# Early-fusion block on one core: full-height table products, high halves read in place, and reordered queues

## The chip, the cores and the metric

One core of one Trainium2 chip. The metric is the device time of one execution in microseconds (us). Several executions are timed and the median is given; one more execution is recorded by the profiler.

## What is computed

The block has three stages. With `x` of 8 x 3 x 512 x 192 and `txt` of 8 x 128 x 192:

```python
h = tokenizer(x)                      # sines and cosines of 6 bands, times W: 8 x 512 x 192
h = concat([h, txt], axis=1)          # 8 x 640 x 192: 40 tiles of 128 tokens
h = h + attention(layernorm(h))
h = h + soft_experts(layernorm(h))

def attention(x):                     # 12 heads of 64, 4 query groups
    k, v = x @ Wk, x @ Wv
    q = ln(gelu((x @ Wq) @ Wt + bt)) * gt + betat       # per group and head, over 64
    qf, kf = phi(q) / sqrt(128), phi(k)                 # phi(u) = [relu(u), relu(-u)]
    kv, ksum = sum_n kf v, sum_n kf                     # one table per batch and head
    out = (qf @ kv) / (qf . ksum + 1e-6)
    return gelu(ln(out @ Wf + bf)) @ Wo + bo
```

Matrix products of float32 are made from bf16 halves: a x b is taken as a_hi b_hi + a_hi b_lo + a_lo b_hi, summed in PSUM.

## The kernel before

`early_fusion_kernel` calls the tokenizer, `attention_weights` (folds Wt into Wq), `keys_and_values`, `attend` and `soft_experts` one after the other. Each writes the instruction streams of the five engines by hand, with semaphores between them; an engine runs its own stream strictly in the order written. The change touches `keys_and_values` and `attend`.

**keys_and_values** goes over 8 batches x 5 tiles x 2 halves of six heads. For each half TensorE projects keys and values into a bank pair of `ps_p` (two sets, one for each half), ScalarE writes `kf` = relu(+k), relu(-k) and `v_hi`, VectorE and GpSimd make `kf_hi`, `kf_lo`, `v_lo`. One half tile later `accumulate` (L521 to L534) sums the tables: for each pair of heads, each sign and each of the three half products, two matmuls, one per head (`side`), with 64 columns of weights each. They write the lower or upper 64 partitions of `ps_kv`, so the table of a head lies on 64 partitions, two signs apart in the free dimension. A 65th column of ones in `v` gives `ksum`. That makes 36 matmuls for each of the 80 half tiles. `store_kv` splits the finished sums into `kvs` (high and low bf16).

**attend** works through 40 tiles x 6 octets (8 heads of the 48 query heads, as 4 pairs) in slots. `slot(tile, j)` exists for each engine, and names in which order that engine touches the neighbouring octets:

- TensorE (from L969): queries of octet j+3 (5 matmuls of 512 columns), at j = 2 `turn_x`, then `turn_octet(j)` (4 f32 transposes of the normalised queries into `ps_t`), at j = 4 `turn_y` of the previous tile (6 transposes), `attend_octet(j-1)`, `fuse(j-2)` (24 matmuls of 384 columns with Wf), `turn_outputs(j-1)` (4 transposes into `ps_u`), at j = 5 `project_out`(18 matmuls).
- ScalarE: `high_outputs(j-2)` (`o_hi`), `gelu(j+3)`, `features(j)` (L1006: `phi` = relu(+-q gt +- betat); one instruction for each sign and query group, so two, or four in octets 1 and 4 in which two groups meet), `square(j+2)`, at j = 4 both parts of `fused_gelu`.
- VectorE: `center(j+2)` (L1090), `low_outputs(j-2)` (`o_lo`, L1134), `sum_q(j+3)`, `divide(j-1)`, `scale_q(j+1)`, `high_phi(j)` (L1112, cast of `phi` to `phi_hi`), `sum_squares(j+2)`; in single slots the layernorms of `x` and `y`, and at j = 5 `high_ys` (L1163).
- GpSimd: `rstd_q(j+1)` (L1221, L1224), `low_phi(j)` (L1231), in single slots `rstd_y` and `low_ys`.

Features of sign +1 and -1 lie apart in the free dimension, and the two heads of a pair on 64 partitions each. So a table product contracts over 64 rows. The two heads go to the two halves of the array's rows and to two banks:

```python
for n, (feature, table) in enumerate(((phi_hi, 0), (phi_hi, 1), (phi_lo, 0))):
    for a in range(2):
        rows = slice(a * DH, (a + 1) * DH)
        last = nc.tensor.matmul(
            ps_o[:, a, i * KVW:(i + 1) * KVW],
            feature[rows, j % 2, sign, i * P:(i + 1) * P], kv_now[rows, table, pair, sign, :],
```

That is 4 pairs x 2 signs x 3 x 2 = 48 matmuls an octet, 65 columns each. `kv_now` holds the tables of the tile's batch: SyncE copies 390 KB in all 40 times from `kvs` by DMA (L854), so that TensorE's operands have fixed addresses. `phi`, `phi_hi` and `phi_lo` have two buffers (j % 2); `ps_t`, `ps_o`, `ps_u` one each. `fuse(j-2)` waits for `o_hi` and `o_lo` of its octet (L935).

The tokenizer, which the change leaves alone, reads high halves in place: `high(r)` (L72) is the float32 tile `feat` seen as bf16, every second element, and goes to L154 as weights; the low halves `f_low` are packed bf16 and go to L163.

## Time and profile before

| | |
|---|---|
| median of 3 runs | 2654.25 us (2653.22 to 2655.28) |
| profiled execution | 2652.76 us |
| its span, first to last instruction | 2651.0 us |
| TensorE busy / VectorE / ScalarE / GpSimd | 94% / 91% / 52% / 51% of the span |
| mean granted TensorE clock | 0.965 of full speed |
| keys_and_values | about 510 to 760 us |
| attend | about 760 to 2530 us |

Engines in the rows below: PE is TensorE's matmuls, PEld its weight loads, DVE VectorE, ACT ScalarE, POOL GpSimd. A matmul's recorded time is a latency and overlaps the next one's, so for TensorE the start times tell the pace. "<-issue" marks idle time in which the engine waited for nothing that the profile shows.

### The profile page before, as it was taken

The page shows a single profiled execution, that of the slowest core. Times are in us where ns is not written, and L with a number is a line of the kernel's source. Part 1 is how long each engine was busy: PE and PEld are TensorE (multiplying, and loading weights), DVE is VectorE, ACT ScalarE, POOL GpSimd, SP SyncE. Part 2 cuts the span into 40 slices and gives each one's busy share as a digit, 9 for nine tenths or more (in the row PEclk, how much of TensorE's full clock was granted, in tenths as well). Part 3 has the DMA queues.
Part 4 walks back from the last instruction along what each step waited for, and adds up shares of the span by engine and source line. Part 5 has one row for each costly group of instructions (what it writes and reads, how often), then busy time and mean ns, then how long its engine had stood idle before and what let it go on. Part 6 is the DMA issues. An engine that isn't in the chain of part 4 may idle for free. (4 is left out here: it accounts for less than half of the span.)

```text
span 2651.0 us, 74429 instructions
## 1 busy us (share of the span) xinstructions
PE 2481.3 (94%) x29338; PEld 1697.5 (64%) x29338; DVE 2419.1 (91%) x3549; ACT 1385.3 (52%) x2270; POOL 1351.4 (51%) x1019
## 2 busy tenths in 40 slices
PE   4999999788879999999999999999999999999946
PEld 2777777555546666666666666666666666666634
DVE  6999999788879999999999999999999999999852
ACT  5677767455554454555545454545454545454441
POOL 0000000455556666666666666666666666666630
PEclk8999999799989999999999999999999999999965
DMA  7421210111100000000000000000000000000001
GB/s 149 105 54 36 53 36 18 51 39 45 36 14 14 7 12 6 12 6 12 6 12 6 12 6 12 6 12 6 12 6 12 6 12 6 12 6 12 8 7 60
DMA packets 45459, 62.41 MB, mean 24 GB/s; under 512 B 4736, under 2 KB 36480, under 8 KB 45080
## 3 DMA queue, kind: packets, MB, share of 16 engines
q1 hardware_dynamic: 44248, 61.09, 8.7%
q8 instruction: 41, 0.67, 0.1%
q10 hardware_dynamic: 1152, 0.51, 0.1%
q14 instruction: 18, 0.15, 0.0%
HBM read 41.67 MB, written 3.93 MB: 17 GB/s over the span
## 5 line engine op out<-in xcount | busy, mean ns | idle before, releaser
L1231 POOL TENSOR_TENSOR phi_lo<-phi,phi_hi 128x1024 bf16<-128x1024 f32 x240 | 511.4, 2131 | 459.8 <-DVE phi_hi L1112 459.8
L1022 ACT ACTIVATE o_hi<-ps_u 128x512 bf16<-128x512 f32 x240 | 143.3, 597 | 706.1 <-PE ps_u L927 706.1
L941 PE MATMUL ps_y<-staging,o_hi 128*128 128x384 bf16 x1920 | 470.7, 327 | 9.8 <-DVE o_lo L1134 1.9
L941 PE MATMUL ps_y<-staging,o_lo 128*128 128x384 bf16 x1920 | 469.3, 326 | 0.0
L941 PE MATMUL ps_y<-wf_lo,o_hi 128*128 128x384 bf16 x1920 | 469.2, 326 | 0.0
L1224 POOL TENSOR_TENSOR q_ssq<-q_ssq,half 128x8 f32<-128x8 f32 x240 | 405.9, 1691 | 18.8
L1013 ACT ACTIVATE phi<-ps_t,betat,gt 128x512 f32<-128x512 f32 (+1 forms) x640 | 384.5, 672 | 0.9 <-PE ps_t L896 0.8
L1090 DVE SCALAR_TENSOR_TENSOR shared<-q_sum,shared 128x512 f32<-128x512 f32 x240 | 374.5, 1560 | 1.4
L154 PE MATMUL acc<-w_b,feat 128*128 128x384 bf16 x1728 | 295.6, 331 | 42.7 <-DVE w_b L266 39.3
L154 PEld LDWEIGHTS acc<-w_b,feat 128*128 128x128 bf16 x1728 | 168.4, 99 | 158.3 <-DVE w_b L266 39.9
L941 PEld LDWEIGHTS ps_y<-staging,o_lo 128*128 128x128 bf16 x1920 | 187.8, 98 | 124.3
L941 PEld LDWEIGHTS ps_y<-wf_lo,o_hi 128*128 128x128 bf16 x1920 | 187.4, 98 | 124.5
L941 PEld LDWEIGHTS ps_y<-staging,o_hi 128*128 128x128 bf16 x1920 | 169.3, 98 | 118.9 <-issue 15.6
L369 POOL MEMSET half<- 128x40 f32 x1 | 0.1, 131 | 476.6 <-POOLq L101 476.6
L252 DVE TENSOR_TENSOR f_low<-feat 128x4608 bf16<-128x4608 f32 x48 | 237.7, 4952 | 1.4 <-ACT feat L196 1.4
L997 ACT ACTIVATE shared<-ps_a 128x512 f32<-128x512 f32 x240 | 143.3, 597 | 179.2 <-PE ps_a L880 176.2
L1112 DVE CAST phi_hi<-phi 128x1024 bf16<-128x1024 f32 x240 | 219.9, 916 | 0.0
L914 PE MATMUL ps_o<-kv_now,phi_hi 64*128 64x65 bf16 x7680 | 212.9, 191 | 1.7 <-issue 1.7
L914 PEld LDWEIGHTS ps_o<-kv_now,phi_hi 64*128 64x128 bf16 x7680 | 183.9, 95 | 42.1 <-issue 42.1
L914 PE MATMUL ps_o<-kv_now,phi_lo 64*128 64x65 bf16 x3840 | 202.8, 190 | 0.0
L1085 DVE TENSOR_REDUCE q_sum<-shared 128x8 f32<-128x512 f32 x240 | 162.5, 677 | 20.8 <-ACT shared L997 19.6
L914 PEld LDWEIGHTS ps_o<-kv_now,phi_lo 64*128 64x128 bf16 x3840 | 180.7, 94 | 0.0
(214 smaller groups left out, 5474.2 us busy)
## 6 DMA issues: line engine op xcount, KB each, us to landing
kv_now<-kvs SPq DMA_DIRECT2D x40, 390.0 KB, 2.6
xt<-in_x_dram SPq DMA_DIRECT2D x32, 320.0 KB, 5.6
wf_f<-in_wf_dram SPq DMA_DIRECT2D x24, 384.0 KB, 3.1
xt<-in_x_dram SPq DMA_DIRECT2D x32, 256.0 KB, 6.0
out_dram<-h SPq DMA_DIRECT2D x8, 480.0 KB, 4.6
staging<-in_wq_t_dram SPq DMA_DIRECT2D x1, 3072.0 KB, 10.5
staging<-in_tok_w_dram SPq DMA_DIRECT2D x12, 192.0 KB, 8.8
staging<-in_kv_w_dram SPq DMA_DIRECT2D x1, 1536.0 KB, 14.9
```

The costliest lines, as they stand in the source:

```text
L154: last = nc.tensor.matmul(acc[:, u, t, 0:2 * DIM], high(ring(u, i))[:, k, t * P:(t + 1) * P], w_b[:, i, k, :], start=i == 0 and k == 0, st ...
L252: nc.vector.tensor_tensor(low[:, r], feat[:, r], high(r), ALU.subtract).then_inc(low_ready, 1)
L914: last = nc.tensor.matmul(ps_o[:, a, i * KVW:(i + 1) * KVW], feature[rows, j % 2, sign, i * P:(i + 1) * P], kv_now[rows, table, pair, sign ...
L941: last = nc.tensor.matmul(ps_y[:, n, 0:HC], lhs, w[part][:, c, n * HC:(n + 1) * HC], start=c == 0 and lhs is oh and part == 'wf_hi', stop= ...
L997: nc.scalar.activation(q[:, j % RING].rearrange("p h d -> p (h d)"), ps_a[:, bank[f"oct{j}"], 0:OC], ACT.Gelu).then_inc(s["gelu_done"], 1)
L1013: last = nc.scalar.activation(phi[:, j % 2, sign, a * P:b * P], ps_t[:, a * P:b * P], ACT.Relu, bias=w['betat'][:, sign, g:g + 1], scale=w ...
L1022: nc.scalar.activation(o_hi[:, j % 2], ps_u[:, 0:OC], ACT.Copy).then_inc(s["o_hi_done"], 1)
L1085: nc.vector.tensor_reduce(total[:, j % 2], q[:, j % RING], AX_X, ALU.add).then_inc(s["q_sum"], 1)
L1090: nc.vector.scalar_tensor_tensor(out=q[:, j % RING], in0=total[:, j % 2].unsqueeze(2).broadcast_to([P, OCT, DH]), scalar=1.0 / DH, in1=q[: ...
L1112: nc.vector.tensor_copy(phi_hi[:, j % 2], phi[:, j % 2]).then_inc(s["phi_hi_done"], 1)
L1224: nc.gpsimd.tensor_tensor(ssq[:, j % 2], ssq[:, j % 2], w['half'][:, 0:OCT], ALU.pow).then_inc(s["q_rstd"], 1)
L1231: nc.gpsimd.tensor_tensor(phi_lo[:, j % 2], phi[:, j % 2], phi_hi[:, j % 2], ALU.subtract).then_inc(s["phi_lo_done"], 1)
```

## The change

- `accumulate` and `attend_octet` use full-height operands: the two signs of one head together make 128 rows. 18 instead of 36 matmuls for each half tile, 24 instead of 48 for each octet, all with 128 x 128 weights and 65 columns. The tables are stored as `kv_hi`, `kv_lo` of [128, batch, head, 65].
- `attend_octet` reads `kv_hi[:, b, hd, :]` and `kv_lo` directly, with the batch `b` computed from the loop's tile; `kv_now`, its DMA and SyncE's stream in `attend` are gone.
- `features` writes one head's plus and minus features on 64 partitions each, which takes an instruction for each head, sign and group: four or eight an octet. `phi_done` rises once for each head.
- `phi_hi` and `ys_hi` become views (upper 16 bits of the float32 elements). `high_phi` and `high_ys` are gone. `low_phi` is two instructions, one for each head of the pairs (128x512 each).
- Orders: ScalarE's `square` goes ahead of `gelu` and `features`, and `fused_gelu(0)` ahead of `features`; VectorE's `sum_squares` goes up behind `low_outputs`, `y_aggregate` up, `normalize_x` from j = 1 to j = 0; TensorE turns the first half of y ahead of `turn_octet` and the second behind `attend_octet`.

```diff
@@ accumulate
-                    for j in range(HH // 2):
-                        for sign in range(2):
-                            for n, (k, v) in enumerate(((kf_hi, v_hi), (kf_hi, v_lo), (kf_lo, v_hi))):
-                                for side in range(2):
-                                    c = 2 * j + sign
-                                    last = nc.tensor.matmul(
-                                        ps_kv[side * DH:(side + 1) * DH, hf, c * KVW:(c + 1) * KVW],
-                                        k[:, m, 2 * j + side, sign, :], v[:, m, 2 * j + side, :],
...
+                    for j in range(HH):
+                        for n, (k, v) in enumerate(((kf_hi, v_hi), (kf_hi, v_lo), (kf_lo, v_hi))):
+                            last = nc.tensor.matmul(ps_kv[:, hf, j * KVW:(j + 1) * KVW],
+                                                    k[:, m, j].rearrange("p s d -> p (s d)"), v[:, m, j, :],
...
@@ attend
+        ys_hi = y.bitcast(BF16)[:, 1::2]
-        kv_now = sb("kv_now", [P, 2, HP, 2, KVW], BF16)
-        phi = sb("phi", [P, 2, 2, PAIRS * P], F32)
-        phi_hi = sb("phi_hi", [P, 2, 2, PAIRS * P], BF16)
-        phi_lo = sb("phi_lo", [P, 2, 2, PAIRS * P], BF16)
+        phi = sb("phi", [P, 2, PAIRS, 2, P], F32)
+        phi_hi = phi[:, :, :, :, :].bitcast(BF16)[:, :, :, :, 1::2]
+        phi_lo = sb("phi_lo", [P, 2, PAIRS, 2, P], BF16)
-        ys_hi = sb("ys_hi", [P, INNER], BF16)
...
-            @block.sync
-                def tables(tile):
-                    if (n := earlier(tile, NO - 1, NO, NO)) is not None:
-                        sp.wait_ge(s["attended"], n)
-                    sp.dma_start(kv_now[:, :, :, :, :], kvs[:, batch_of(tile.t)]).then_inc(s["kv_in"], 16)
...
                 def attend_octet(tile, j):
-                    pe.wait_ge(s["phi_hi_done"], count(tile, j, NO))
-                    pe.wait_ge(s["phi_lo_done"], count(tile, j, NO))
                     if (n := earlier(tile, j, NO, 1)) is not None:
                         pe.wait_ge(s["o_done"], n)
-                    if j == 0:
-                        pe.wait_ge(s["kv_in"], 16 * count(tile, 0, 1))
...
+                    b = batch_of(tile.t)
+                    for n in range(OCT):
+                        if n % PAIRS == 0:
+                            pe.wait_ge(s["phi_lo_done"], count(tile, 2 * j + n // PAIRS, 2 * NO))
+                        i = 2 * (n % PAIRS) + n // PAIRS
+                        hd = (OCT * j + i) % HEADS
+                        c = i % PAIRS
+                        out = ps_o[:, i // PAIRS, c * KVW:(c + 1) * KVW]
+                        ph, pl = (v[:, j % 2, i // 2, i % 2, :] for v in (phi_hi, phi_lo))
+                        nc.tensor.matmul(out, ph, kv_hi[:, b, hd, :], start=c == 0, stop=False, skip_group_check=True)
+                        nc.tensor.matmul(out, ph, kv_lo[:, b, hd, :], start=False, stop=False, skip_group_check=True)
+                        last = nc.tensor.matmul(out, pl, kv_hi[:, b, hd, :], start=False, stop=c == PAIRS - 1,
+                                                skip_group_check=True)
...
@@ TensorE slot
+                    if j == 4 and tile.prev().real:
+                        turn_y(tile.prev(), 0, tile)
                     if tile.real:
                         turn_octet(tile, j)
-                    if j == 4 and tile.prev().real:
-                        turn_y(tile.prev(), tile)
                     of, k = octet(tile, j - 1)
                     if of.real:
                         attend_octet(of, k)
+                    if j == 4 and tile.prev().real:
+                        turn_y(tile.prev(), 1, tile)
@@ ScalarE
-                        act.wait_ge(s["phi_hi_done"], n)
-                        act.wait_ge(s["phi_lo_done"], n)
-                    for sign in range(2):
+                        act.wait_ge(s["attended"], n)
+                    for head in range(2):
+                        rows = slice(head * DH, (head + 1) * DH)
                         for g, a, b in groups(j):
-                            last = nc.scalar.activation(
-                                phi[:, j % 2, sign, a * P:b * P], ps_t[:, a * P:b * P], ACT.Relu,
-                                bias=w['betat'][:, sign, g:g + 1], scale=w['gt'][:, sign, g:g + 1])
-                    last.then_inc(s["phi_done"], 1)
+                            for sign in range(2):
+                                last = nc.scalar.activation(
+                                    phi[sign * DH:(sign + 1) * DH, j % 2, a:b, head, :],
+                                    ps_t[rows, a * P:b * P].rearrange("p (i n) -> p i n", n=P), ACT.Relu,
+                                    bias=w['betat'][rows, sign, g:g + 1], scale=w['gt'][rows, sign, g:g + 1])
+                        last.then_inc(s["phi_done"], 1)
...
@@ GpSimd
-                    nc.gpsimd.tensor_tensor(phi_lo[:, j % 2], phi[:, j % 2], phi_hi[:, j % 2],
-                                            ALU.subtract).then_inc(s["phi_lo_done"], 1)
+                    for head in range(2):
+                        pool.wait_ge(s["phi_done"], count(tile, 2 * j + head, 2 * NO))
+                        nc.gpsimd.tensor_tensor(phi_lo[:, j % 2, :, head], phi[:, j % 2, :, head], phi_hi[:, j % 2, :, head],
+                                                ALU.subtract).then_inc(s["phi_lo_done"], 1)
```

## Rows read from the trace of the kernel before

**Rows 1.** Busy us by stage (PE, PEld, DVE, ACT, POOL, clock, DMA): two windows.

```profile
510.00:777.00 267.00, 224.07 (x3795) 143.50 (x3795) 216.71 (x434) 144.26 (x335) 143.08 (x136) 0.93 0.12 38
1200.00:2400.00 1200.00, 1194.42 (x14688) 808.61 (x14687) 1166.19 (x1809) 595.35 (x1149) 805.05 (x576) 1.00 0.02 9
```

**Rows 2.** Who waited for whom, 1200 to 2400 us (total us, times, longest).

```profile
POOL phi_lo L1231 <- DVE phi_hi L1112: 315.3, 138, 4.2
PEld ps_o L914 <- issue: 27.3, 164, 0.2
PEld ps_a L952 <- ACT shared L997: 6.1, 27, 0.2
```

**Rows 3.** Timeline of TensorE through one octet (start us, us, engine, line, ...).

```profile
1300.49 0.60 PE L896 MATMUL ps_t<-ident,z 128*128 128x128 f32 x4
1301.02 0.24 PE L914 MATMUL ps_o<-kv_now,phi_hi 64*128 64x65 bf16 x4
...
1301.75 0.19 PE L914 MATMUL ps_o<-kv_now,phi_lo 64*128 64x65 bf16 x2
1301.87 0.50 PE L941 MATMUL ps_y<-staging,o_hi 128*128 128x384 bf16 x2
...
1305.78 0.60 PE L927 MATMUL ps_u<-ident,o 128*128 128x128 f32 x4
1306.22 0.38 PE L876 MATMUL ps_a<-q_hi,xh 128*128 128x512 bf16 x1
```

**Rows 4.** Timeline of TensorE: once a tile, and two tiles 43.73 us apart.

```profile
1307.30 0.38 PE L887 MATMUL ps_a<-ident,xn 128*128 128x128 f32 x2
...
1308.77 0.19 PE L914 MATMUL ps_o<-kv_now,phi_lo 64*128 64x65 bf16 x2
1309.04 0.49 PE L941 MATMUL ps_y<-staging,o_hi 128*128 128x384 bf16 x2
...
1334.86 0.25 PE L962 MATMUL ps_a<-wo_hi,ys_hi 128*128 128x192 bf16 x1
...
1336.34 0.38 PE L876 MATMUL ps_a<-q_hi,xh 128*128 128x512 bf16 x1
...
1351.03 0.38 PE L887 MATMUL ps_a<-ident,xn 128*128 128x128 f32 x2
```

**Rows 5.** Timeline of VectorE: the low half that `fuse` at 1309.04 us reads.

```profile
1308.26 0.68 DVE L1134 TENSOR_TENSOR o_lo<-ps_u,o_hi 128x512 bf16<-128x512 f32 x1
```

**Rows 6.** Weight loads of the whole run by line and shape.

```profile
L914 PEld LDWEIGHTS ps_o<-kv_now,phi_lo 64*128 64x128 bf16 x3840 | 180.7, 94 | 0.0
L154 PEld LDWEIGHTS acc<-w_b,feat 128*128 128x128 bf16 x1728 | 168.4, 99 | 158.3 <-DVE w_b L266 39.9 <-ACT feat L195 7.4 <-issue 7.0
L163 PEld LDWEIGHTS acc<-w_b,f_low 128*128 128x128 bf16 x1728 | 144.0, 98 | 6.1
L927 PEld LDWEIGHTS ps_u<-ident,o 128*128 128x128 f32 x960 | 120.4, 142 | 21.9 <-DVE o L1126 1.4
```

**Rows 7.** Timeline of TensorE through one half tile of keys and values.

```profile
603.75 0.22 PE L529 MATMUL ps_kv<-v_hi,kf_hi 128*64 128x65 bf16 x2
...
604.31 0.20 PE L529 MATMUL ps_kv<-v_hi,kf_lo 128*64 128x65 bf16 x2
604.44 0.34 PE L510 MATMUL ps_p<-shared,xh 128*128 128x384 bf16 x1
```

**Rows 8.** Groups of VectorE and GpSimd, 1200 to 2400 us.

```profile
L1112 DVE CAST phi_hi<-phi 128x1024 bf16<-128x1024 f32 x165 | 153.9, 933 | 0.0
L1231 POOL TENSOR_TENSOR phi_lo<-phi,phi_hi 128x1024 bf16<-128x1024 f32 x165 | 351.6, 2131 | 315.3 <-DVE phi_hi L1112 315.3
```

**Rows 9.** Timeline of ScalarE: features in two and in four instructions, gelu of y.

```profile
1301.18 1.93 ACT L1013 ACTIVATE phi<-ps_t,betat,gt 128x256 f32<-128x256 f32 x4
...
1308.41 1.44 ACT L1013 ACTIVATE phi<-ps_t,betat,gt 128x512 f32<-128x512 f32 x2
...
1324.53 2.22 ACT L1037 ACTIVATE shared<-ps_a,betaf,gf 128x128 f32<-128x128 f32 x6
```

More of the change, by code:

```diff
@@ L439, in keys_and_values @@
     HH = HEADS // 2
-    PH = HH // 2
     HC = HH * DH
@@ L705, in _, with attend @@
                     batch(b, False)
-def attend(nc, w, shared, kvs, stats, h, ident):
+def attend(nc, w, shared, kv_hi, kv_lo, stats, h, ident):
     OCT = 8
@@ L892, in turn_octet @@
                     pe.wait_ge(s["q_scaled"], count(tile, j, NO))
-                    if (n := earlier(tile, j, NO, 1)) is not None:
+                    if (n := earlier(tile, 2 * j, 2 * NO, 1)) is not None:
                         pe.wait_ge(s["phi_done"], n)
@@ L901, in attend_octet @@
                 def attend_octet(tile, j):
-                    pe.wait_ge(s["phi_hi_done"], count(tile, j, NO))
-                    pe.wait_ge(s["phi_lo_done"], count(tile, j, NO))
                     if (n := earlier(tile, j, NO, 1)) is not None:
                         pe.wait_ge(s["o_done"], n)
-                    if j == 0:
-                        pe.wait_ge(s["kv_in"], 16 * count(tile, 0, 1))
-                    for i in range(PAIRS):
-                        pair = (PAIRS * j + i) % HP
-                        for sign in range(2):
-                            for n, (feature, table) in enumerate(((phi_hi, 0), (phi_hi, 1), (phi_lo, 0))):
-                                for a in range(2):
-                                    rows = slice(a * DH, (a + 1) * DH)
-                                    last = nc.tensor.matmul(
-                                        ps_o[:, a, i * KVW:(i + 1) * KVW],
-                                        feature[rows, j % 2, sign, i * P:(i + 1) * P], kv_now[rows, table, pair, sign, :],
-                                        start=i == 0 and sign == 0 and n == 0,
-                                        stop=i == PAIRS - 1 and sign == 1 and n == 2, skip_group_check=True)
+                    b = batch_of(tile.t)
[11 more added lines that the diff above has]
+                                                skip_group_check=True)
                     last.then_inc(s["attended"], 1)
@@ L1044, in slot @@
                         high_outputs(of, k)
+                    of, k = octet(tile, j + 2)
+                    if of.real:
+                        square(of, k)
                     of, k = octet(tile, j + 3)
@@ L1049, in slot @@
                         move_x(tile.next())
+                    if j == 4 and tile.prev().real:
+                        fused_gelu(tile.prev(), 0)
                     if tile.real:
                         features(tile, j)
-                    of, k = octet(tile, j + 2)
-                    if of.real:
-                        square(of, k)
                     if j == 4 and tile.prev().real:
-                        fused_gelu(tile.prev(), 0)
                         fused_gelu(tile.prev(), 1)
@@ L1106, in scale_q @@
                                             ALU.mult).then_inc(s["q_scaled"], 1)
-                def high_phi(tile, j):
-                    dve.wait_ge(s["phi_done"], count(tile, j, NO))
-                    if (n := earlier(tile, j, NO, 2)) is not None:
-                        dve.wait_ge(s["attended"], n)
-                    nc.vector.tensor_copy(phi_hi[:, j % 2], phi[:, j % 2]).then_inc(s["phi_hi_done"], 1)
                 def divide(tile, j):
@@ L1157, in normalize_y @@
                     nc.vector.tensor_scalar(y, y, yst[:, 0:1], yst[:, 1:2], ALU.subtract, ALU.mult).then_inc(s["y_norm"], 1)
-                def high_ys(tile):
-                    dve.wait_ge(s["ys_done"], count(tile, 1, 2))
-                    if (n := earlier(tile, 0, 1, 1)) is not None:
-                        dve.wait_ge(s["out_proj"], n)
-                    nc.vector.tensor_copy(ys_hi[:, :], ys).then_inc(s["ys_hi_done"], 1)
                 def add_to_h(tile):
@@ L1183, in slot @@
                         low_outputs(of, k)
+                    if j == 3 and prev.real:
+                        y_aggregate(prev)
                     if j == 0 and prev.prev().real:
                         add_to_h(prev.prev())
+                    of, k = octet(tile, j + 2)
+                    if of.real:
+                        sum_squares(of, k)
                     if j == 2 and nxt.real:
@@ L1200, in slot @@
                         scale_q(of, k)
-                    if tile.real:
-                        high_phi(tile, j)
-                    of, k = octet(tile, j + 2)
-                    if of.real:
-                        sum_squares(of, k)
                     if j == 2 and prev.real:
```

63 lines of the change are left out of this document (25 added, 38 removed).

## The prediction

> **What bounds the kernel now.** I read the windows by stage first, then the list of waits, then TensorE's timeline, and in the last the start times, since recorded matmul times overlap. From 1200 to 2400 us TensorE is busy 1194 of 1200 us at full granted clock, which is the 2.4 GHz level [rows 1]. VectorE is at 97%, ScalarE at 50%, GpSimd at 67%. The long waits belong to engines that wait for work, such as GpSimd for `phi_hi` [rows 2]. So TensorE's own order of instructions sets the pace, and a tile takes 1351.03 - 1307.30 = 43.73 us [rows 4]; there are 40 tiles. The pieces of a tile:
>
> - five query matmuls 1306.22 to 1307.30: 1.08; four transposes 1305.78 to 1306.22: 0.44, twice; `fuse` 1301.87 to 1305.78: 3.91. Six times 5.87 is 35.2 us.
> - once a tile, two and six more transposes at 0.11 (0.22 and 0.65) and `project_out`, 1334.86 to 1336.34: 1.48. Sum 2.35.
> - the table products of an octet, first product to `fuse`: 0.85. The transposes ahead of them take 0.53 instead of 0.44 (1300.49 to 1301.02), so 0.09 goes on entering. Together 0.94, six times 5.66 [rows 3].
>
> That is 43.2 us. The remaining 0.5 us are short waits: of `fuse` for `o_lo` (0.27 instead of 0.12 after the last product, `o_lo` ending at 1308.94) [rows 4, 5], and of `turn_y` for `gelu`, 6.1 us in 27 tiles, 0.2 each [rows 2]. In keys and values TensorE is busy 224 of 267 us [rows 1]: the bound there changes between it and the chain over ScalarE and VectorE.
>
> **Part 1, table products in attend.** Now 24 pairs start 0.032 us apart (1301.02 to 1301.75 for 23 steps), two 64-row matmuls side by side, and 0.09 is lost on entering and as much on leaving (0.12 from the last start to `fuse`) [rows 3]. That loss comes where the shape changes from full height to half height; with full-height products it should vanish. What 24 single products cost, each with a 128x128 load and 65 columns, no row shows. Lower bound: full-height products take 0.163 us at 384 columns (3.91/24) and 0.082 at 192 (1.48/18) [rows 3, 4], a line of 0.00042 us a column, which gives 0.029 at 65. Upper bound: 0.082, the shortest pace at which a full-height load is seen. I take 0.031, near the line, because loads of 128 columns at 64 rows already follow each other every 0.032 us in each half of the array, and 128 rows do not lengthen a load much (94 against 98 ns). The strided high half does not either: the tokenizer's strided `feat` loads take 99 ns, the packed `f_low` 98, while float32 loads show 142 [rows 6]. So 24 x 0.031 = 0.74 against 0.94: -0.20 x 240 octets = **-48 us** (at 0.029: -60; at 0.082: +245).
>
> **Part 2, the short waits.** 0.5 us x 40 = 21 us are there to win. `o_lo` is late because VectorE has no slack. The change takes the casts of `phi` (0.93 us each, six a tile) [rows 8] and of `ys` off VectorE, some 6 us of a tile. The second half of y is turned only after the products, by when `gelu` is done. I take two thirds: **-14** (0 to -21).
>
> **Part 3, more work elsewhere, costed at nothing.** Features took 1.44 us (two instructions) or 1.93 (four) [rows 9]. With twice as many of the same length it is about 2.8 and 3.7 us, +9 us a tile for ScalarE, which then works about 31 of 42 us. Its fullest slot is j = 4: three instructions of 0.6 at most (a 512-column feature takes 0.7), 3.7 of features, 2.2 of gelu of y [rows 9], 7.7 us against a TensorE slot of 5.87 + 0.65 + 0.74 = 7.3. The next slot has room, and `o_hi` is due only after 2.3 us of it. `low_phi` in two pieces costs GpSimd between 2.1 us (the same elements) [rows 8] and twice that; I take 2.6. It needs no `phi_hi` any more, a wait of 315 us in 1200 [rows 2]. Chain of an octet: transposed 2.0 us into its slot, first head done at 3.5 to 4, its low half at 5.2, the second low half at 6.2 to 7.1; the products want them at 6.6 (a slot, 5.87 + 0.74) + 1.5 (queries and transposes), the second 0.4 later. Cover of one microsecond or more; if it goes, each microsecond late in each octet costs 240 us. `turn_octet` now waits for both heads of the octet before; ScalarE is done with them at 5 to 6. `square` ahead of `gelu` waits for VectorE's `center`, and `gelu` and `features` are queued behind it. `center` depends on work of the slot before and comes first in VectorE's slot; if it came late all the same, that is rival A.
>
> **Part 4, tables.** `kv_now`'s DMA was hidden behind an octet: nothing. In its place TensorE's queue computes addresses: 16 an octet, high and low of eight heads. The page doesn't count register instructions. Lower bound nothing; upper bound 0.17 us each, the longest "issue" wait of TensorE (27.3 us in 164) [rows 2]. I take nothing, since TensorE's queue runs ahead as soon as `phi_lo` is there, over a microsecond before the products are due.
>
> **Part 5, keys and values.** A half tile's tables cost 0.69 (603.75 to 604.44) [rows 7] and an entry of 0.09; 18 x 0.031 is 0.56. 0.22 x 80 = 18 us where TensorE is the bound. It waits for others in the rest, and nothing in their chain gets shorter, so I take **-7** (0 to -18). Ends of attend: **-1**, from the two casts that leave the last chain.
>
> **Sum.** Against the profiled execution's 2652.8 us: -48 - 14 - 7 - 1 = -70, so 2583. The median of the runs is 1.5 us above that execution: **2584 us**. A tile should take 42.2 us or a little less.
>
> **Rivals.**
> A, the forecast side but smaller: a new wait (ScalarE's full slot j = 4, or `center` held by the low halves) stands on TensorE's path once a tile. Half a microsecond to one and a half, 20 to 60 us, gives 2604 to 2644. For it: both engines get tighter or more entangled there. Against: the cover above. Chance 0.15.
> B, slower: the weight load isn't hidden behind 65 columns. It sits in the products of both stages and decides from 24 X = 0.94 + the waits won, X = 0.043 us. If 128 columns enter at the line's pace, X is 128 x 0.00042 + 0.002 = 0.056: +96 us in attend, +9 in keys and values, -15, so 2744; if only the 16 strided loads of an octet do so, +48 - 7 - 15, so 2680. Against: half-height loads at a 0.032 us pace and 99 against 98 ns [rows 3, 6]. For: no full-height load is seen closer than 0.082. Chance 0.10.
> The Trainium skill ("TensorE: Matmul & The Clock Gate", section "Back-to-back issue gap") speaks for B: it gives 81 ns for each load and matmul pair at 128 columns, against 56 by its formula without the load. The same 25 ns on top of 65 columns would give 54 ns and a time near 2735. At 192 columns this trace is at 82 ns, which is its formula with no load on top; at 65 nothing here shows it.
> C, slower: TensorE's queue is not ahead, and the 16 addresses stand in the open. At 0.1 us each (between the bounds) 1.6 us go by in which 0.74 of products run: +0.86 in 222 octets of the loop, 2775. It decides from 0.3 us exposed an octet. Chance 0.07.
> D, no gain: pairs were as good as singles (X = 0.033 is -35 already), and new waits eat the rest. Chance 0.04.
>
> **Chances.** Forecast 0.64 (2562 to 2604), A 0.15, B 0.10, C 0.07, D 0.04. A measurement of this kernel tells 0.2%, 5 us, from no change. Faster 0.79, same 0.04, slower 0.17. The lower end is X = 0.029 with all waits gone and full gain in keys and values, 2560; the upper end takes in A and reaches D: 2655. B and C, 0.17, are left out.
>
> **What would show it.** Right: tile 42.2 us; products 0.03 us apart, with no 0.09 at either end; loads of `phi` at 98 ns; `fuse` 0.03 to 0.16 after the last product. Rival A: a TensorE wait for `o_hi`, `o_lo` or `ps_t` in slot 4 or 5. B: even spacing of 0.05 or more. C: uneven spacing, with "issue" ahead of every new table. In keys and values, `ps_p` waits that grow while the products shrink would show the -7 as right. The prediction is wrong if the spacing of the products is over 0.035, or if VectorE or ScalarE turns out to be the one that never waits.

## The result, and the profile after

The changed kernel takes 2595.92 us (median of 4 runs, 2593.07 to 2596.41) against 2654.77 for the kernel before on the same chip: ratio 0.9775, 95% interval 0.9762 to 0.9788. The forecast was 2584, the range 2560 to 2655. The profiled execution took 2596.41 us, 56.4 less than that of before. From the traces: the last product of keys and values starts at 754.05 us instead of 758.24 (-4.2), from there to the last table product it takes 1706.4 us instead of 1756.8 (-50.4), and the rest is 1.8 shorter. So nine tenths of the gain lie in `attend`'s loop. The kernel before was timed again beside each group of experiments; its medians lie between 2653.93 and 2655.15 us, so times of different groups can be compared to about 1 us. One execution of experiment 9 took 14106 us, five times as long as its three others, and is left out there.

The busy windows of the changed kernel (PE, PEld, DVE, ACT, POOL, clock, DMA), beside [rows 1]:

```profile
510.00:756.00 246.00, 202.69 (x2320) 139.06 (x2320) 207.27 (x420) 135.61 (x320) 137.72 (x130) 0.94 0.12 39
1200.00:2400.00 1200.00, 1178.20 (x10914) 831.81 (x11083) 961.19 (x1672) 943.16 (x1639) 789.31 (x765) 1.00 0.00 0
```

From 1200 to 2400 us VectorE fell from 97% to 80%, ScalarE rose from 50% to 79%. TensorE's 1178 is too low by records that are missing: of an octet's first query product (L860) only 4 of 240 are in this trace. Its timeline through one octet, beside [rows 3]:

```profile
1300.12 0.60 PE L880 MATMUL ps_t<-ident,z 128*128 128x128 f32 x4
1300.56 0.19 PE L897 MATMUL ps_o<-kvs_hi,phi 128*128 x1
1300.59 0.20 PE L898 MATMUL ps_o<-kvs_lo,phi 128*128 x1
1300.62 0.19 PE L899 MATMUL ps_o<-kvs_hi,phi_lo 128*128 x1
...
1301.25 0.20 PE L899 MATMUL ps_o<-kvs_hi,phi_lo 128*128 x1
1301.28 0.52 PE L933 MATMUL ps_a<-ident,shared 128*128 128x128 f32 x3
```

The products start 0.03 us apart, whether the left operand is the strided high half or the packed low half, and the next work follows 0.03 after the last. The 0.09 lost on entering and on leaving is gone: from the first transpose to the first product it is 0.44. An octet's products take 1301.28 - 1300.56 = 0.72 us, not 0.85, or 0.94 with the loss on entering. Once a tile, one slot later, it looks different; beside [rows 4], with two tiles 42.48 us apart:

```profile
1308.19 0.19 PE L899 MATMUL ps_o<-kvs_hi,phi_lo 128*128 x1
1308.85 0.32 PE L923 MATMUL ps_y<-staging,o_hi 128*128 128x384 bf16 x1 [0.47 <-DVE o_lo L1113]
...
1328.91 0.38 PE L871 MATMUL ps_a<-ident,xn 128*128 128x128 f32 x2
...
1371.39 0.38 PE L871 MATMUL ps_a<-ident,xn 128*128 128x128 f32 x2
```

`fuse` stands 0.66 us behind the last product instead of 0.03. The list of waits from 1200 to 2400 us has the same, once in each of 28 tiles (beside [rows 2]):

```profile
POOL phi_lo L1200 <- ACT phi L996: 395.9, 311, 2.9
DVE o_lo L1113 <- ACT o_hi L1006: 141.2, 84, 4.1
PEld ps_y L923 <- issue: 15.5, 28, 0.6
PE ps_y L923 <- DVE o_lo L1113: 12.9, 28, 0.5
```

`o_lo` itself had waited 4.1 us for `o_hi`. VectorE's row (beside [rows 5]) and ScalarE's timeline of slot j = 4 and the start of the next (beside [rows 9]):

```profile
1308.02 0.69 DVE L1113 TENSOR_TENSOR o_lo<-ps_u,o_hi 128x512 bf16<-128x512 f32 x1 [4.14 <-ACT o_hi L1006]
```

```profile
1298.91 0.60 ACT L1006 ACTIVATE o_hi<-ps_u 128x512 bf16<-128x512 f32 x1 [1.39 <-PE ps_u L909]
1299.69 0.63 ACT L986 ACTIVATE shared<-shared 128x512 f32<-128x512 f32 x1 [0.18 <-DVE shared L1075]
1300.23 0.58 ACT L979 ACTIVATE shared<-ps_a 128x512 f32<-128x512 f32 x1
1300.71 1.15 ACT L1021 ACTIVATE shared<-ps_a,betaf,gf 128x128 f32<-128x128 f32 x3
1301.73 4.58 ACT L996 ACTIVATE phi<-ps_t,betat,gt 64x256 f32<-64x256 f32 x8
1306.34 1.16 ACT L1021 ACTIVATE shared<-ps_a,betaf,gf 128x128 f32<-128x128 f32 x3
1307.38 0.60 ACT L1006 ACTIVATE o_hi<-ps_u 128x512 bf16<-128x512 f32 x1
```

ScalarE has no gap from 1299.69 on: the eight feature instructions take 4.58 us, the second half of y's gelu stands behind them, and `o_hi` of the next octet starts only at 1307.38, though its input has been there since 1306.14, the end of the transposes that started at 1305.54. Groups by line and shape, beside [rows 6, 8]:

```profile
L1200 POOL TENSOR_TENSOR phi_lo<-phi 128x512 bf16<-128x512 f32 x339 | 356.2, 1051 | 395.9 <-ACT phi L996 395.9
L996 ACT ACTIVATE phi<-ps_t,betat,gt 64x512 f32<-64x512 f32 x454 | 350.1, 771 | 6.0
L996 ACT ACTIVATE phi<-ps_t,betat,gt 64x256 f32<-64x256 f32 x449 | 250.7, 558 | 6.0
L897 PEld LDWEIGHTS ps_o<-kvs_hi,phi 128*128 128x128 bf16 x1360 | 125.4, 97 | 0.0
L899 PEld LDWEIGHTS ps_o<-kvs_hi,phi_lo 128*128 128x128 bf16 x1360 | 124.8, 98 | 0.0
```

Loads of strided and packed weights both take 97 to 98 ns. A low half in two pieces costs GpSimd 2 x 1.05 = 2.1 us, as before. Keys and values, a half tile (beside [rows 7]):

```profile
605.45 0.19 PE L525 MATMUL ps_kv<-v_hi,kf_hi 128*128 128x65 bf16 x1
...
605.97 0.19 PE L525 MATMUL ps_kv<-v_hi,kf_lo 128*128 128x65 bf16 x1
606.30 0.32 PE L509 MATMUL ps_p<-shared,xh 128*128 128x384 bf16 x1
```

18 products in 0.55 us instead of 0.69, but here 0.3 us pass before the next projection.

### The profile page after: what moved, and what is told of

Same layout as the page of the kernel before. It is cut to its first block and busy times, and to the rows that moved or that the text cites. A ratio compares the mean times of both kernels' runs of the same rounds, so it can differ in the third digit from the quotient of the medians.

```text
span 2594.6 us, 61547 instructions
## 1 busy us (share of the span) xinstructions
PE 2397.1 (92%) x21902; PEld 1695.1 (65%) x22138; DVE 2081.3 (80%) x3269; ACT 1849.9 (71%) x2910; POOL 1294.7 (50%) x1259
## 5 line engine op out<-in xcount | busy, mean ns | idle before, releaser
L996 ACT ACTIVATE phi<-ps_t,betat,gt 64x512 f32<-64x512 f32 (+1 forms) x1280 | 850.9, 665 | 17.1
L1200 POOL TENSOR_TENSOR phi_lo<-phi 128x512 bf16<-128x512 f32 x480 | 506.9, 1056 | 557.2 <-ACT phi L996 557.2
L1113 DVE TENSOR_TENSOR o_lo<-ps_u,o_hi 128x512 bf16<-128x512 f32 x240 | 164.5, 685 | 213.8 <-ACT o_hi L1006 213.8
L1089 DVE TENSOR_TENSOR z<-shared,q_ssq 128x512 f32<-128x512 f32 x240 | 246.1, 1026 | 0.0
L1075 DVE SCALAR_TENSOR_TENSOR shared<-q_sum,shared 128x512 f32<-128x512 f32 x240 | 207.4, 864 | 1.4
L898 PE MATMUL ps_o<-kvs_lo,phi 128*128 (+1 forms) x1920 | 199.5, 193 | 0.0
L897 PE MATMUL ps_o<-kvs_hi,phi 128*128 (+1 forms) x1920 | 199.2, 193 | 0.2
L899 PE MATMUL ps_o<-kvs_hi,phi_lo 128*128 (+1 forms) x1920 | 198.5, 193 | 0.0
L190 ACT ACTIVATE near<-xt,fr 128x2304 int32<-128x2304 f32 x48 | 106.4, 2218 | 129.0 <-DVE feat L236 122.8
L986 ACT ACTIVATE shared<-shared 128x512 f32<-128x512 f32 x240 | 151.9, 633 | 61.8 <-DVE shared L1075 59.5
```

The lines of the kernel that those rows point to most:

```text
L897: nc.tensor.matmul(out, ph, kv_hi[:, b, hd, :], start=c == 0, stop=False, skip_group_check=True)
L898: nc.tensor.matmul(out, ph, kv_lo[:, b, hd, :], start=False, stop=False, skip_group_check=True)
L899: last = nc.tensor.matmul(out, pl, kv_hi[:, b, hd, :], start=False, stop=c == PAIRS - 1, skip_group_check=True)
L996: last = nc.scalar.activation(phi[sign * DH:(sign + 1) * DH, j % 2, a:b, head, :], ps_t[rows, a * P:b * P].rearrange("p (i n) -> p i n", n ...
L1075: nc.vector.scalar_tensor_tensor(out=q[:, j % RING], in0=total[:, j % 2].unsqueeze(2).broadcast_to([P, OCT, DH]), scalar=1.0 / DH, in1=q[: ...
L1089: nc.vector.tensor_tensor(z[:, j % 2], q[:, j % RING], ssq[:, j % 2].unsqueeze(2).broadcast_to([P, OCT, DH]), ALU.mult).then_inc(s["q_scal ...
```

## The experiments

**1. The gelu that stands in the way, one slot later.** The changed kernel with one edit in ScalarE's order:

```diff
                     if of.real:
                         high_outputs(of, k)
+                    if j == 5 and tile.prev().real:
+                        fused_gelu(tile.prev(), 1)
...
-                    if j == 4 and tile.prev().real:
-                        fused_gelu(tile.prev(), 1)
```

> The changed kernel, with the gelu of the second half of y moved on ScalarE from the end of slot 4 to slot 5, right behind the high halves of the outputs. Theory S (ScalarE's fullest slot makes o_hi late once a tile, so o_lo and TensorE's fuse are late): TensorE's wait for o_lo, 0.63 us a tile, goes; a tile falls from 42.48 to about 41.85 us and the time from 2596 to about 2571 us. Rival V (VectorE or GpSimd holds o_lo, or the later gelu makes the output projection wait for ys_lo by as much): the wait stays or moves to the projection, 2590 to 2600 us.

Measured: 2572.76 us (2571.81 to 2575.03), ratio to the kernel before 0.9694 (0.9678 to 0.9710), as all ratios below. Its window and ScalarE's timeline:

```profile
1200.00:2400.00 1200.00, 1200.00 (x11242) 842.36 (x11240) 951.18 (x1692) 961.15 (x1664) 800.97 (x776) 1.00 0.00 0
```

```profile
1295.90 3.44 ACT L996 ACTIVATE phi<-ps_t,betat,gt 64x256 f32<-64x256 f32 x6
1299.36 0.60 ACT L1006 ACTIVATE o_hi<-ps_u 128x512 bf16<-128x512 f32 x1
1299.99 1.16 ACT L1021 ACTIVATE shared<-ps_a,betaf,gf 128x128 f32<-128x128 f32 x3
```

The features stay as long (six of the eight are in this view), but `o_hi` goes ahead of the gelu. TensorE has no wait left in 1200 us, and a tile is 41.87 us. So the wait of `fuse` cost 42.48 - 41.87 = 0.61 us a tile, 24 us by that sum and 23 by the times, and the order of two ScalarE steps was its cause. It also gives the sum of TensorE's work alone: of the 43.73 us before, 41.87 + 6 x 0.22 = 43.19 were work and 0.54 waits.

**2. Half as many feature instructions.** The changed kernel with one instruction on 128 partitions for each head and group; it leaves out that a head's rows go to both halves, so positive and negative features are mixed between two heads:

```diff
-                            for sign in range(2):
-                                last = nc.scalar.activation(
-                                    phi[sign * DH:(sign + 1) * DH, j % 2, a:b, head, :],
-                                    ps_t[rows, a * P:b * P].rearrange("p (i n) -> p i n", n=P), ACT.Relu,
+                            last = nc.scalar.activation(
+                                phi[:, j % 2, a:b, head, :],
+                                ps_t[:, a * P:b * P].rearrange("p (i n) -> p i n", n=P), ACT.Relu,
...
```

> The changed kernel, with half the feature instructions: one instruction of 128 partitions for each head slot and group in place of two of 64 partitions. It leaves out that each half of the partitions gets its own head and sign, so the features are those of the kernel before in the new places. Theory S: ScalarE has some 10 us a tile less to do, the wait for o_lo goes, tile 41.85 us, about 2571 us. Rival V: ScalarE was not the cause, the tile stays at 42.4 to 42.5 us, 2594 us.

Measured: 2573.11 us (2571.65 to 2574.03), ratio 0.9695 (0.9678 to 0.9711); tile 41.87, no TensorE wait, ScalarE 620 of 1200 us. The same wait goes when only the features get shorter: its two causes together, the length and the order, are confirmed from both sides.

**3. Is it the crossing of partitions?** The same number of instructions, each writing the 64 partitions that it reads (it leaves out the same as experiment 2):

```diff
-                            for sign in range(2):
+                            for side in range(2):
+                                rows = slice(side * DH, (side + 1) * DH)
                                 last = nc.scalar.activation(
-                                    phi[sign * DH:(sign + 1) * DH, j % 2, a:b, head, :],
+                                    phi[rows, j % 2, a:b, head, :],
...
```

> The changed kernel in which each feature instruction writes the same 64 partitions that it reads (as many instructions of the same sizes in the same order; it leaves out that a head's rows go to both halves, so positive and negative features are mixed between two heads). In the changed kernel half of them write to the other 64 partitions. Theory: an activation that crosses to the other partitions is the longer one, and explains why four take 3.13 us and eight 4.58 where 2.8 and 3.7 were estimated: here four take 2.7 to 2.9 us and eight 3.6 to 3.9, o_hi of the next slot is in time, the tile falls to about 41.9, total 2572 to 2580. Rival: the length belongs to an instruction with 64 partitions (or this form of one) wherever it writes: 3.13 and 4.58 as in the changed kernel, tile 42.4 to 42.5, total 2593 to 2599.

Measured: 2594.27 us (2593.59 to 2594.95), ratio 0.9773 (0.9757 to 0.9790), tile 42.48 us. The theory fell. The group of ScalarE here, and the same in experiment 2:

```profile
L997 ACT ACTIVATE phi<-ps_t,betat,gt 64x512 f32<-64x512 f32 x453 | 349.3, 771 | 6.0
L997 ACT ACTIVATE phi<-ps_t,betat,gt 64x256 f32<-64x256 f32 x450 | 251.3, 559 | 6.0
```

```profile
L995 ACT ACTIVATE phi<-ps_t,betat,gt 128x512 f32<-128x512 f32 x230 | 165.5, 774 | 0.0
L995 ACT ACTIVATE phi<-ps_t,betat,gt 128x256 f32<-128x256 f32 x228 | 110.4, 582 | 0.0
```

One instruction lasts about as long on 64 partitions as on 128. What differs is how close the next one follows. Four of 128x256 took 1.93 us [rows 9], so they started (1.93 - 0.58) / 3 = 0.45 us apart, each before the one ahead had ended. Eight of 64x256 take 4.58: (4.58 - 0.56) / 7 = 0.57 apart, one after the other. For 512 columns it is 0.67 against 0.79. It isn't the new layout of `phi` either: experiment 2 writes to the same places with 128 partitions, and there four of 256 columns take 1.95 us and two of 512 take 1.44, as before. Why those of 64 partitions don't overlap isn't settled: in both kernels neighbours write alternately to the two halves of the partitions, and an order without that was not tried.

**4. All the old orders.** The changed kernel with the orders of TensorE, ScalarE and VectorE as before:

```diff
@@ ScalarE
-                        square(of, k)
...
-                        fused_gelu(tile.prev(), 0)
...
                         features(tile, j)
+                        square(of, k)
+                        fused_gelu(tile.prev(), 0)
@@ VectorE
-                        y_aggregate(prev)
...
-                        sum_squares(of, k)
...
                         divide(of, k)
+                        y_aggregate(prev)
...
                         scale_q(of, k)
+                        sum_squares(of, k)
...
-                    if j == 0 and nxt.real:
+                    if j == 1 and nxt.real:
                         normalize_x(nxt)
@@ TensorE
-                        turn_y(tile.prev(), 0, tile)
...
                         turn_octet(tile, j)
+                        turn_y(tile.prev(), 0, tile)
+                        turn_y(tile.prev(), 1, tile)
...
                         attend_octet(of, k)
-                        turn_y(tile.prev(), 1, tile)
```

> The changed kernel with the orders of the kernel before on all engines (square behind features, both halves of gelu of y behind square, y turned in one piece ahead of the products, sum of squares last, normalize_x in slot 1). If the product part makes the gain and the orders little: TensorE's wait in turn_y (0.2 us a tile) comes back and the one for o_lo stays, 2600 to 2612 us. Rival O (the orders are needed because the doubled feature work needs them): several waits of TensorE a tile, tile over 43.2 us, 2625 us or more. If the orders do nothing: 2596 us.

Measured: 2673.55 us (2671.82 to 2673.91), ratio 1.0070 (1.0053 to 1.0087), tile 44.43 us. Without the new orders the change would have been a loss. From its list of waits:

```profile
DVE q_ssq L1083 <- ACT shared L986: 180.3, 135, 2.8
PEld ps_a L871 <- issue: 28.5, 27, 1.1
PEld ps_a L860 <- ACT shared L1021: 26.0, 27, 1.0
```

`square` stands behind features of 3.1 or 4.6 us, VectorE's `sum_squares` waits for it, and what VectorE does after that comes late: TensorE waits a microsecond a tile for `xn` (L871; VectorE's step ends the wait). It waits as long again with the next queries (L860) for a bank that y's gelu (L1021) clears, since both gelus stand last on ScalarE. The two waits are 2.0 of the 2.6 us by which this tile is longer than one without waits.

**5. Old orders, half as many feature instructions.** Experiments 2 and 4 together, and so with what experiment 2 leaves out:

```diff
+                                phi[:, j % 2, a:b, head, :],
...
                         features(tile, j)
+                        square(of, k)
+                        fused_gelu(tile.prev(), 0)
...
```

> All orders of before, with the features in half as many instructions (128 partitions each; it leaves out that each head's rows go to both halves, so positive and negative features are mixed between two heads). Theory: the new orders are needed only because the features' instructions doubled; with half of them the old orders lose little: tile 42.0 to 42.6, 2577 to 2600, against 2673.6 with the doubled ones. Rival: the old orders cost by themselves (the short waits of the kernel before were theirs, and casts off VectorE don't end them): tile 43 or more, 2620 or more.

Measured: 2577.38 us (2575.65 to 2578.09), ratio 0.9711 (0.9696 to 0.9726), tile 42.05 us. With short features the old orders cost 4 us, with the doubled ones 78 (2673.55 - 2595.92). The orders are there for the features' length.

**6. ScalarE's old order alone.** The ScalarE part of the edit of experiment 4:

```diff
-                        square(of, k)
...
-                        fused_gelu(tile.prev(), 0)
...
                         features(tile, j)
+                        square(of, k)
+                        fused_gelu(tile.prev(), 0)
```

> The changed kernel, with the old order on ScalarE alone (features ahead of square, both gelus of y last). With all old orders it was 2673.6 us. Theory A (ScalarE's order makes it: the sum of squares waits behind 3.1 to 4.6 us of features, and VectorE's stream, in order, waits with it): 2640 us or more, the wait of VectorE's q_ssq for ScalarE long. Rival W (VectorE's and TensorE's orders make it, since normalize_x and the aggregate stood behind the sum of squares): 2596 to 2615 us.

Measured: 3263.56 us (3262.47 to 3282.89), ratio 1.2317 (1.2286 to 1.2348), a tile of 57 to 61 us. Far slower than all old orders together. Its waits:

```profile
DVE q_ssq L1083 <- ACT shared L986: 566.8, 121, 5.5
PE ps_u L909 <- DVE o L1105: 251.7, 121, 3.0
```

In VectorE's new order `sum_squares` comes ahead of `sum_q`, the division and the scaling. Behind ScalarE's old order it waits for `square` in each octet, 4.7 us in the mean, with all of these queued behind it; then TensorE waits for `o`, and the engines go one after the other. The mean granted clock from 1200 to 2400 us is 0.94 here instead of 1.00, which adds to it. The direction had been expected, the size by far not.

**7. TensorE's and VectorE's old orders, ScalarE's new one.** The VectorE and TensorE parts of that edit:

```diff
                         divide(of, k)
+                        y_aggregate(prev)
...
                         scale_q(of, k)
+                        sum_squares(of, k)
...
                         turn_octet(tile, j)
+                        turn_y(tile.prev(), 0, tile)
+                        turn_y(tile.prev(), 1, tile)
```

> The changed kernel with TensorE's and VectorE's orders of before, but ScalarE's new order (square ahead of the features, gelu of y on both sides of them). It splits the 78 us that all the old orders cost, and the run with ScalarE's old order alone gave 3264. Theory S (it is ScalarE's square that must not stand behind the doubled features; the two other orders are small): tile 42.3 to 42.9 us, 2590 to 2612. Rival T (VectorE's early sums and TensorE's split turn of y carry half or more): tile 43.4 or more, 2635 to 2680, with a wait of turn_octet for center or of turn_x for xn on TensorE.

Measured: 2653.89 us (2652.71 to 2656.38, 10 runs), ratio 0.9998 (0.9989 to 1.0007), tile 43.96 us. The time is in the rival's range, but the wait is one that neither named:

```profile
1316.23 0.49 PE L933 MATMUL ps_a<-ident,shared 128*128 128x128 f32 x3
1318.03 0.55 PE L933 MATMUL ps_a<-ident,shared 128*128 128x128 f32 x3 [1.31 <-ACT shared L979]
```

```profile
1316.86 0.63 ACT L986 ACTIVATE shared<-shared 128x512 f32<-128x512 f32 x1 [1.35 <-DVE shared L1075]
```

The second half of y needs the bank that `gelu` (L979) clears. In the old order it stands ahead of the products, some 1.5 us a tile in the open; in the new order the products and their 0.72 us stand between. They would cover only half of this wait. `gelu` itself is late: it stands behind `square` (L986), which waits 1.35 us for VectorE's `center` (L1075). `center` ends at 1316.83, 1.04 us after TensorE has begun the octet's transposes (1315.79); in the changed kernel it ends 0.46 before them. So rival T's `center` is in the chain, though the wait shows elsewhere. The three orders work as one piece here; TensorE's and VectorE's were not tried apart.

**8. The new orders alone, on the kernel before.** The reverse of experiment 4's edit, with `turn_y` split and the casts kept:

```diff
+                        square(of, k)
...
+                        fused_gelu(tile.prev(), 0)
                         features(tile, j)
...
-                        square(of, k)
...
-                        fused_gelu(tile.prev(), 0)
                         fused_gelu(tile.prev(), 1)
...
+                        sum_squares(of, k)
...
                         scale_q(of, k)
...
-                        sum_squares(of, k)
...
```

> The kernel before, with the new orders alone (square and sum of squares early, y turned and its gelu in two parts, normalize_x in slot 0). Theory P (before, the orders had almost nothing to win: TensorE's waits were 0.54 us a tile; they are needed only for the doubled features): at most those waits go, 2633 to 2650 us. Rival O (the orders are worth their 78 us in any kernel): 2580 to 2600 us. Third: VectorE, still with its casts, gets later by the early sums and it is slower than 2655 us.

Measured: 2689.64 us (2687.49 to 2690.97), ratio 1.0133 (1.0117 to 1.0148), tile 44.63 us:

```profile
POOL phi_lo L1233 <- DVE phi_hi L1114: 368.1, 162, 3.7
PEld ps_o L914 <- issue: 36.5, 162, 0.6
PEld ps_a L951 <- ACT shared L998: 19.8, 27, 0.7
```

This is the third of the outcomes named. While VectorE still has the casts, sums moved ahead make `phi_hi` later, GpSimd waits 368 us for it instead of 315 [rows 2], and TensorE for the low halves (36.5 us ahead of the products instead of 27.3; in one slot of a tile they start 0.38 us later than in the others, 0.10 behind the end of the low half). `turn_y` waits longer for `gelu`, too, 19.8 us instead of 6.1. The orders gain nothing by themselves.

**9. The high half by a cast again.** The changed kernel with `phi_hi` as a packed buffer of its own, written by VectorE, and `low_phi` behind it:

```diff
-        phi_hi = phi[:, :, :, :, :].bitcast(BF16)[:, :, :, :, 1::2]
+        phi_hi = sb("phi_hi", [P, 2, PAIRS, 2, P], BF16)
...
+                    nc.vector.tensor_copy(phi_hi[:, j % 2], phi[:, j % 2]).then_inc(s["phi_hi_done"], 1)
...
+                    pool.wait_ge(s["phi_hi_done"], count(tile, j, NO))
                     for head in range(2):
-                        pool.wait_ge(s["phi_done"], count(tile, 2 * j + head, 2 * NO))
```

> The changed kernel, with phi_hi made again by a VectorE cast of both heads into packed bf16, GpSimd's low halves behind it. If the strided view costs TensorE nothing: products 29 to 31 ns apart as in the changed kernel. The cast costs VectorE 5.6 us a tile and delays the low halves by 1 to 2 us in each octet: tile 42.5 to 43.5 us, 2597 to 2637 us. Rival (the view is only a saving of VectorE work that was off the path): 2594 to 2597 us. Rival B of the prediction: the packed loads are closer together than the strided ones.

Measured: 2800.71 us (2799.03 to 2801.51, 3 runs), ratio 1.0546 (1.0527 to 1.0566):

```profile
POOL phi_lo L1208 <- DVE phi_hi L1097: 439.5, 151, 4.8
DVE phi_hi L1097 <- ACT phi L996: 155.1, 101, 3.1
PE ps_o L897 <- POOL phi_lo L1208: 75.4, 124, 1.3
```

```profile
1320.00:1326.00 6.00, 4.17 (x46) 2.79 (x45) 3.62 (x8) 5.91 (x12) 3.65 (x4) 0.99 0.00 0
1326.00:1329.00 3.00, 3.00 (x11) 1.49 (x10) 2.85 (x3) 1.09 (x2) 2.16 (x2) 0.50 0.00 0
```

All expectations missed. Where TensorE doesn't wait, the products keep their 0.03 us with packed operands, so the view costs TensorE nothing. But features, cast and low half one after another are longer than the slots allow, and TensorE waits in the products. The view is not a saving on the side: it takes a step of the chain away that the longer features need. How much of the 205 us a cast must cost is not settled: here one cast of both heads stands behind `scale_q`, so the low half of the first head waits for the second head too; a cast for each head, or another place for it, was not tried. The last two rows are of two windows in sequence: TensorE is busy 4.17 of 6 us, and in the 3 us after them the granted clock is at the 1.2 GHz level (0.50). From 1200 to 2400 us it is 0.98 in the mean; [rows 1] and the changed kernel have 1.00 there.

**10. Fixed table addresses.** The changed kernel with `b = 0` in `attend_octet`; it leaves out that later batches read their own tables:

```diff
-                    b = batch_of(tile.t)
+                    b = 0
```

> The changed kernel with the batch number fixed at 0 in the table products, so that TensorE's operands have fixed addresses; it leaves out that later batches use their own tables. If computing the addresses is hidden: same time as the changed kernel, 2594 to 2597 us, products 29 to 30 ns apart in both. Rival C of the prediction (computed addresses stand in the open in part): faster by 5 us or more, with more even spacing.

Measured: 2600.24 us (2598.93 to 2601.06), ratio 0.9795 (0.9779 to 0.9811), the products 0.03 us apart as before. No gain (against both expectations it is 4 us slower, by a slightly longer wait of `fuse` for `o_lo`, a tile of 42.59 us; why isn't known): TensorE's queue computes its 16 addresses under cover.

**11. The products of keys and values alone.** The kernel before with full-height products there and nothing else; its tables then don't lie as `attend` reads them, which leaves the right values out of the attention:

```diff
-                                for side in range(2):
-                                    c = 2 * j + sign
...
+                            last = nc.tensor.matmul(ps_kv[:, hf, j * KVW:(j + 1) * KVW],
+                                                    k[:, m, j].rearrange("p s d -> p (s d)"), v[:, m, j, :],
...
```

> The kernel before, with the 18 full-height products in keys and values alone; it leaves out that the tables then lie where attend looks for them. Products take 0.55 instead of 0.69 us a half tile and the 0.09 ahead of them goes; the wait for ps_p takes most of it back: 2648 to 2652 us, first query about 4 us earlier (the changed kernel: 758.8 instead of 762.6 us). Rival: where TensorE was the bound for all 80 half tiles, 2637 us.

Measured: 2646.11 us (2644.57 to 2646.81), ratio 0.9965 (0.9952 to 0.9979), 9 us less than the 2655.15 beside it and a little below the expected range. The profiled executions differ by 6.3 us, and the last product of keys and values starts at 751.84 us (before 758.24), 6.4 sooner; the tile is unchanged at 43.73.

**12. A version that beats both.** Experiment 1, and the same idea once more: in keys and values the high half of `kf` as a view, four buffers for `kf`, no cast:

```diff
-        kf = sb("kf", [P, 2, HH, 2, DH], F32)
-        kf_hi = sb("kf_hi", [P, 4, HH, 2, DH], BF16)
+        kf = sb("kf", [P, 4, HH, 2, DH], F32)
+        kf_hi = kf[:, :, :, :, :].bitcast(BF16)[:, :, :, :, 1::2]
...
-                    nc.vector.tensor_copy(kf_hi[:, m], kf[:, hf]).then_inc(kf_hi_ready, 1)
```

> The changed kernel with gelu of y's second part one slot later (as in the run that took 2572.8) and, new, the high half of the keys' features in keys and values read by view too: the features get four buffers, VectorE's cast kf_hi goes. Theory: keys and values are bound in part by VectorE's chain (the products' pace there fell by more than the time did), so the cast's time comes back where TensorE waits for projected halves: first query at 735 to 750 us instead of 758.8, tile unchanged at 41.87, total 2550 to 2566. Rival: ScalarE's or GpSimd's part of the chain, or the projections, are the bound there: first query within 2 us of 758.8, total 2571 to 2575.

Measured: 2548.45 us (2547.93 to 2549.28, 5 runs), ratio 0.9603 (0.9590 to 0.9616), 24 us less than experiment 1 and a little below the expected range; last product of keys and values at 728.08 us instead of 754.05 (752.33 in experiment 1), tile 41.87. The window of keys and values:

```profile
510.00:730.00 220.00, 198.32 (x2320) 136.94 (x2319) 160.56 (x335) 134.75 (x320) 128.06 (x130) 0.95 0.13 44
```

Beside the window shown first, TensorE does the same 2320 matmuls in 26 us less, and VectorE has 47 us less to do. In the changed kernel the projections waited for VectorE:

```profile
PE ps_p L509 <- DVE v_lo L638: 15.8, 17, 1.3
```

Here this wait is 0.2 us. So VectorE's chain kept the gain of the shorter products small. The edit also gives `kf` four buffers instead of two, and ScalarE no longer waits for the low halves before it writes the next `kf` (14.4 us in the changed kernel); how much of the 24 us each part brings was not tried.

## Why the prediction was right, and where it wasn't

**What bounds the kernel: right.** TensorE's order of work, 43.2 us of it and 0.5 of waits; by experiment 1 they are 43.19 and 0.54.

**Part 1, -48: right in mechanism and nearly in size.** X = 0.030 us, no loss at either end: 0.72 against 0.94 is 0.22 x 240 = -53. The line through the paces at 384 and 192 columns gave 0.029 at 65. Rival B (the load not hidden, 0.043 or more) fell with it. The Trainium skill ("TensorE: Matmul & The Clock Gate", "Back-to-back issue gap") has 81 ns for a pair of load and matmul at 128 columns, 25 more than without a load. At 65 columns these traces show 29 to 36, 30 in the mean. That is the pace of the line, with nothing on top, so the page's extra 25 ns is not seen here.

**Part 2, -14: wrong, +3.** Waits went from 0.54 to 0.61 us a tile. VectorE did get its slack (97% to 80%), and the old waits went. The step that failed is in Part 3, "costed at nothing": "features about 2.8 and 3.7 us" were 3.13 and 4.58, since the estimate took the pace of 128-partition instructions (0.67 and 0.45) for those on 64 (0.79 and 0.57). In slot j = 4 that is 0.9 us. The text had 7.7 us of ScalarE's work in that slot against 7.3 of TensorE's; from its `o_hi` (1298.91) to the next (1307.38) it was 8.5. `o_hi` had to start by 1306.75 to keep `fuse` at 1308.22 (1308.22 less 0.14 between the end of `o_lo` and `fuse`, 0.69, 0.04 and 0.60); it started 0.63 late, and with 3.7 us of features it would have been in time by 0.25. This is rival A in mechanism and place ("ScalarE's full slot j = 4", half a microsecond or more, shown by an `o_lo` wait in slot 5), worth 24 us. The time still lies among those given to the forecast (2562 to 2604), and that is partly luck: rival A's wait came true beside the forecast, and Part 1 brought 5 us more than costed. Without that wait it would have been near 2573.

**Part 3, the rest.** GpSimd's two pieces cost 2.1 us, not 2.6. No wait stood in the chain of the low halves, though the cover was thin: at 1307.43 the second low half ended that the products read from 1307.86 on. What the text did not see is how much it took to keep these waits away: the orders are worth 78 us beside the doubled features, the missing cast, as experiment 9 places it, some 200.

**Part 4, nothing: right.** Experiment 10; rival C fell. (The 0.17 us that the text took as an upper bound is the mean of 27.3 us in 164 waits; the longest is 0.2.)

**Part 5, -7, and the ends, -1: right within what can be told.** The last product of keys and values started 4.2 us sooner; in the ten other runs with the same products and casts there it started at 751.1 to 754.2, 4 to 7 us sooner than before (experiment 8, with the products of before, has 761.4). The predicted sign, waits of `ps_p` that grow while products shrink, was there: TensorE's wait for `v_lo` is 15.8 us where the kernel before has 9.4. The ends gave 1.8.

**Sum.** -53 + 3 - 4.2 - 1.8 = -56, against -70. One sum of the text is off: the lower end of its range, by its own terms (-60 - 21 - 18 - 1), is 2554 and not 2560.

## What to carry to other kernels

Doubling the instructions of an engine with half its time free can still put it on the critical path in its fullest slot; cost them by their spacing, not by the length of another shape's, and write each slot's due times out. When the operations of one engine get longer, its order and the orders of those that wait for it have to change together: parts of such a set, tried alone, were level with the kernel before or up to 23% slower. A high half read as a view removes a link of the chain as well as a cast, and the same edit is worth looking for in the other stages (24 us here, with more buffers).

## What the runs showed of the hardware that was not expected

- Activations of 64 partitions last as long as those of 128 (771 and 774 ns for 512 columns) but follow each other 0.79 us apart instead of 0.67 (0.57 instead of 0.45 for 256), whether they cross to the other partitions or not.
- A matmul with 65 columns and a full 128x128 load starts every 0.03 us, with strided weights as with packed ones, and in front of and behind it work of the same height follows with no gap; two half-height matmuls side by side had cost 0.032 and 0.09 on entering and on leaving.
- One engine's wait put ahead of its other work can make the engines go one after the other: 3263 us for an order that differs in two places on ScalarE.
